# Queries projected as [feature, token] and rotated by three engines, in a fused attention and expert layer on one core

## What is computed

```python
h = concat(tokens_of_image(x), txt)                   # (4, 768, 192)
h = h + attention(layernorm(h))
h = h + ffn(layernorm(h))

# attention: H = 6 heads, DQK = 128, DV = 64
Q = xpos((x @ Wq).reshape(B, T, H, 128), +1)          # x1*cos - x2*sin, x1*sin + x2*cos
K = xpos((x @ Wk).reshape(B, T, H, 128), -1)          # x1, x2: the two halves of the 128 features
V = (x @ Wv).reshape(B, T, H, 64)
out = (Q @ K.T * 128 ** -0.5 * causal_decay_mask) @ V
out = group_norm(out) * silu(x @ Wg) @ Wo
```

## Time and profile before

| | |
|---|---|
| time, median of 3 runs | 920.6 us (918.74 to 922.23) |
| the profiled execution's own time | 925.56 us |
| span from its first to its last instruction | 923.7 us |
| attention, all pairs | until 326 us |
| first matmul of the expert loop | 375 us |
| mean granted TensorE clock | 0.98 of full |

### The profile page before, as it was taken

How to read it: one execution, slowest core, us unless ns; L and a number is a source line. 1 busy time by engine, 2 the same in 40 slices (tenths; PEclk the granted TensorE clock), 3 DMA queues, 4 the chain that set the end, 5 groups by cost and what they waited for, 6 DMA issues and landing times.

```text
span 923.7 us, 16126 instructions
## 1 busy us (share of the span) xinstructions
PE 879.9 (95%) x5422; PEld 399.8 (43%) x5422; DVE 663.0 (72%) x1657; ACT 567.5 (61%) x844; POOL 474.4 (51%) x445
## 2 busy tenths in 40 slices
PE   8899999999999988899799999999999999999997
PEld 3477777777678766222222222222232223222222
DVE  6566555665667577677687888788878887877774
ACT  1121211225332354688788798889988897988784
POOL 0335343333335523476756666757575756574452
PEclk8999999999999999699999999999999999999999
DMA  9600002000000096768687888888988888889773
GB/s 246 230 1 1 2 1 74 1 1 1 1 1 16 15 143 159 188 209 267 181 245 229 254 246 268 242 267 236 295 226 270 247 278 224 276 252 290 243 251 100
DMA packets 89805, 154.14 MB, mean 167 GB/s; under 512 B 30212, under 2 KB 56069, under 8 KB 89330
## 3 DMA queue, kind: packets, MB, share of 16 engines
q1 hardware_dynamic: 89236, 151.48, 54.9%
q10 hardware_dynamic: 486, 1.62, 1.2%
HBM read 138.81 MB, written 15.83 MB: 167 GB/s over the span
## 4 chain that ended last, share of the span: by engine, by line
PE 75%; ACT 8%; DMA 5%; DVE 5%; issue 3%; POOL 2%; SPq 1%; ACTq 0%; DVEq 0%; POOLq 0%
PE ps L854 16%; PE ps L791 15%; PE ps L495 9%; PE ps L503 5%; PE ps L830 5%; PE ps L568 4%; PE ps L560 3%; PE ps L577 3%; DMA w_parts<-wp 2%; ACT ring L1168 2%; PE ps L538 2%; DMA wbc<-w_rows 1%; PE ps L590 1%; PE ps L621 1%; PE ps L642 1%
## 5 line engine op out<-in xcount | busy, mean ns | idle before, releaser
L1829 POOL TENSOR_TENSOR ring<-ring,wbc 128x512 f32<-128x512 f32 x192 | 245.0, 1278 | 160.5 <-ACT ring L1179 147.6
L1628 DVE TENSOR_TENSOR ring<-ps,ring 128x1024 f32<-128x1024 f32 x192 | 234.6, 1222 | 85.8 <-PE ps L830 57.1
L791 PE MATMUL ps<-zst,w1st 99*128 99x512 bf16 x768 | 213.9, 389 | 14.7 <-ACT ring L1168 7.2
L854 PE MATMUL ps<-ring,w2cur 128*32 128x512 f32 x1536 | 205.8, 609 | 0.0
L1168 ACT ACTIVATE ring<-ps 128x1024 f32<-128x1024 f32 x192 | 196.7, 1025 | 4.2 <-PE ps L791 4.1
L1690 POOL TENSOR_TENSOR t<-t 128x768 f32<-128x768 f32 x48 | 87.5, 1834 | 189.7 <-DVE t L1310 189.7
L1181 ACT ACTIVATE ps<-ps 128x512 f32<-128x512 f32 x192 | 113.2, 589 | 61.2 <-PE ps L791 60.7
L1631 DVE TENSOR_TENSOR ring<-ps,wbc 128x512 f32<-128x512 f32 x192 | 130.8, 682 | 1.6 <-DMA wbc<-w_rows 1.5
L1308 DVE TENSOR_TENSOR t<-ps,rope 128x768 f32<-128x768 f32 x48 | 45.7, 953 | 107.1 <-PE ps L503 70.5
L791 PEld LDWEIGHTS ps<-zst,w1st 99*128 99x128 bf16 x768 | 60.9, 98 | 140.8 <-issue 38.3
L1179 ACT ACTIVATE ring<-ps 128x512 f32<-128x512 f32 x192 | 116.3, 606 | 0.0
(11 more groups left out here) (173 smaller groups left out, 1121.4 us busy)
## 6 DMA issues: line engine op xcount, KB each, us to landing
wbc<-w_rows SPq DMA_DIRECT2D x192, 512.0 KB, 5.3
w2cur<-in_w SPq DMA_DIRECT2D x48, 256.0 KB, 4.4
w_parts<-wp SPq DMA_DIRECT2D x72, 64.0 KB, 3.1
zst<-z_parts SPq DMA_DIRECT2D x72, 64.0 KB, 4.7
wst<-w_parts SPq DMA_DIRECT2D x24, 128.0 KB, 3.9
z_parts<-zp SPq DMA_DIRECT2D x6, 384.0 KB, 5.3
wst<-w_parts SPq DMA_DIRECT2D x24, 96.0 KB, 3.7
out_h<-h SPq DMA_DIRECT2D x12, 192.0 KB, 5.0
```

The lines of the kernel that those rows point to most:

```text
L791: return pe.matmul(bank(to), w1st[0:99, 4 * a + j, col:col + P], zst[0:99, (i // 2) % 2, j, :], start=True, stop=True)
L854: mm = pe.matmul(bank(YBANK, 0, 512, 32 * j, 32 * j + 32), w2cur[:, n, j, :], ring[:, (4 * g + j) % RING, :], start=False, stop=(n == 7 an ...
L1628: dve.tensor_tensor(v, ps[:, WBANK * 512:WBANK * 512 + 1024], v, ALU.mult).then_inc(s["duo_done"], 1)
L1829: pool.tensor_tensor(ring[:, slot, :], ring[:, slot, :], wbc[:, g % 4, 1, :], ALU.mult).then_inc(s["tri_done"], 1)
```

## The change

Queries are no longer made as rows of tokens and turned, but come out of the projection as [feature, token]. The weights in the array are now the six 128-column blocks of Wq, and the tokens of both tiles stream through at once, 256 columns a pass. Block e (a head) lies at `query_block(e)` in PSUM: heads 0 to 2 at columns 0 to 767, heads 3 to 5 at 1280 to 2047, so that the rests in the upper half of the array (heads 0 to 2) and those in the lower half (heads 3 to 5) never write into one bank together. For the rests the 64 remaining token features must lie in both halves of the partitions for each tile, so `xn` gets four blocks, the last two with those features written twice, and `xn_turn` makes four transposes.

VectorE calls `rotate_queries` for half 1 first, then for half 0. With features along the partitions, the swap of the feature halves crosses partitions. ScalarE does it with two copies of 64 partitions for each half of the heads (`swap`), VectorE multiplies by the cosines (`rotate_queries`), GpSimd multiplies the swapped ones by the sines (`swapped_queries`) and adds (`rotated_queries`). The rope table of the queries is transposed on the host. `turn`, `keep` and `kT` are for keys alone; `heads` waits for `aq` now. `keys` for x=0 waits for both cosine products, for x=1 for both swaps. `t1`, `t2` and `qkT` are split into parts for queries and keys, and `xnT` moves into the space of `zT`.

```diff
-            def queries(k, x):
+            def query_block(e):
+                return e // 3 * 1280 + e % 3 * 2 * P
+
+            def queries(k, half):
                 pe.wait_ge(s["xn_e"], k + 1)
                 if k > 0:
-                    pe.wait_ge(s["g_out" if x else "v_out"], 2 * k)
-                whole(2 * x, k, x, 0, QK)
+                    pe.wait_ge(s["g_out" if half else "v_out"], 2 * k)
+                for e in range(3 * half, 3 * half + 3):
+                    at = query_block(e)
+                    pe.matmul(ps[:, at:at + 2 * P], wcat[:, 0, e * P:e * P + P],
+                              xnT[:, k % 2, 0:2, :].rearrange("p x n -> p (x n)"),
+                              start=(at % 512 == 0 or e == 3), stop=False, skip_group_check=True)
+
+            def query_rests(k):
+                for n in range(3):
+                    for half in range(2):
+                        e = 3 * half + n
+                        at = query_block(e)
+                        mm = pe.matmul(ps[:, at:at + 2 * P], wcat[D2 * half:D2 * half + D2, 1, e * P:e * P + P],
+                                       xnT[D2 * half:D2 * half + D2, k % 2, 2:4, :].rearrange("p x n -> p (x n)"),
+                                       start=False, stop=True, skip_group_check=True)
+                mm.then_inc(s["q_full"], 1)
...
             def keys(k):
...
                 for x in range(2):
-                    pe.wait_ge(s["rq"], 2 * k + x + 1)
+                    if x == 0:
+                        pe.wait_ge(s["rq"], 2 * k + 2)
+                    else:
+                        pe.wait_ge(s["sq"], 2 * k + 2)
                     whole(2 * x, k, x, QK, QK)
...
             def turn(k, x):
-                pe.wait_ge(s["aq"], 2 * k + x + 1)
                 pe.wait_ge(s["ak"], 2 * k + x + 1)
...
-                for kind in range(2):
-                    for e in range(H):
-                        col = 4 * 512 + (kind * H + e) * P
-                        mm = pe.transpose(ps[:, col:col + P], t1[:, 2 * x + kind, e, :], ident[:, :])
+                for e in range(H):
+                    col = 4 * 512 + (x * H + e) * P
+                    mm = pe.transpose(ps[:, col:col + P], t1k[:, x, e, :], ident[:, :])
...
             def heads(k, x):
                 pe.wait_ge(s["kept"], 2 * k + 2)
+                pe.wait_ge(s["aq"], 2 * k + 2)
...
+            def swap(k, x):
+                hd = DQK // 2
+                src = ps[:, 1280 * x:1280 * x + QK].rearrange("p (h n) -> p h n", n=P)
+                act.wait_ge(s["q_full"], k + 1)
+                if x == 1:
+                    act.wait_ge(s["rq"], 2 * k + 1)
+                if k > 0:
+                    act.wait_ge(s["aq"], 2 * (k - 1) + x + 1)
+                act.copy(s2q[0:hd, x, :, :], src[hd:P, :, :])
+                act.copy(s2q[hd:P, x, :, :], src[0:hd, :, :]).then_inc(s["sq"], 1)
...
+            def rotate_queries(k, x):
+                c = k % CH
+                src = ps[:, 1280 * x:1280 * x + QK].rearrange("p (h n) -> p h n", n=P)
+                dve.wait_ge(s["q_full"], k + 1)
+                if x == 0:
+                    dve.wait_ge(s["sq"], 2 * k + 1)
...
+                dve.tensor_tensor(t1q[:, x, :, :], src, _mid(rope[:, c, 0, :], H), ALU.mult).then_inc(s["rq"], 1)
...
+            def swapped_queries(k, x):
+                pool.wait_ge(s["sq"], 2 * k + x + 1)
...
+                pool.tensor_tensor(s2q[:, x, :, :], s2q[:, x, :, :], _mid(rope[:, k % CH, 1, :], H),
+                                   ALU.mult).then_inc(s["mq"], 1)
+
+            def rotated_queries(k, x):
+                pool.wait_ge(s["rq"], 2 * k + 2)
+                pool.wait_ge(s["mq"], 2 * k + 2)
+                if k > 0:
+                    pool.wait_ge(s["at_full"], 2 * k)
+                pool.tensor_tensor(qT[:, x, :, :].rearrange("p h n -> p (h n)"),
+                                   t1q[:, x, :, :].rearrange("p h n -> p (h n)"),
+                                   s2q[:, x, :, :].rearrange("p h n -> p (h n)"), ALU.add).then_inc(s["aq"], 1)
```

More of the change, by code:

```diff
@@ L155, in fused_layer @@
             state = alloc(region, "state", [P, 2, 2, H, DV])
-            xn = alloc(region, "xn", [P, 3, P])
-            xnT = alloc(region, "xnT", [P, 2, 3, P])
-            xim = t1[0:IMG, 0:2, :, :].rearrange("p a h d -> p (a h d)")[:, 0:B * CIN * IMG]
+            xn = alloc(region, "xn", [P, 4, P])
+            xnT = zT[:, 3 * BLK:5 * BLK].rearrange("p (b x n) -> p b x n", b=2, x=4)
+            xim = t1q[0:IMG, :, :, :].rearrange("p h a n -> p (h a n)")[:, 0:B * CIN * IMG]
             picked = pT[:, :, :, :].rearrange("p a h d -> p (a h d)")[:, 0:B * CIN * IMG]
@@ L486, in xn_turn @@
                 pe.wait_ge(s["xn_d"], k + 1)
-                for n in range(3):
+                for n in range(4):
                     mm = pe.transpose(bank(7, n * P, n * P + P), xn[:, n, :], ident[:, :])
@@ L543, in gates @@
                         mm = pe.matmul(bank(2 + x, g * P, g * P + P), wcat[D2 * x:D2 * x + D2, 1, col:col + P],
-                                       xnT[D2 * x:D2 * x + D2, k % 2, 2, :], start=False, stop=True,
+                                       xnT[D2 * x:D2 * x + D2, k % 2, 2 + x, :], start=False, stop=True,
                                        skip_group_check=True)
@@ L565, in heads @@
                 pe.wait_ge(s["kept"], 2 * k + 2)
+                pe.wait_ge(s["aq"], 2 * k + 2)
                 for e in range(H):
                     col = 4 * 512 + (x * H + e) * P
-                    mm = pe.matmul(ps[:, col:col + P], qkT[:, x, H + e, :], qkT[:, x, e, :], start=True, stop=True)
+                    mm = pe.matmul(ps[:, col:col + P], kT[:, x, e, :], qT[:, e // 3, e % 3 * 2 + x, :], start=True, stop=True)
                 mm.then_inc(s["sc"], 1)
@@ L576, in sums @@
                     o = bank(4 + x, 384 + e * DV, 448 + e * DV) if e < 2 else bank(6, x * 256 + (e - 2) * DV, x * 256 + (e - 1) * DV)
-                    mm = pe.matmul(o, t1[:, 2 * x + 1, e, :], vn[:, x, e, :], start=True, stop=True)
+                    mm = pe.matmul(o, t1k[:, x, e, :], vn[:, x, e, :], start=True, stop=True)
                 mm.then_inc(s["st_full"], 1)
@@ L592, in outputs @@
                             else:
-                                mm = pe.matmul(o, state[:, k % 2, x, 2 * g + e, :], qkT[:, x, 2 * g + e, :],
+                                mm = pe.matmul(o, state[:, k % 2, x, 2 * g + e, :], qT[:, (2 * g + e) // 3, (2 * g + e) % 3 * 2 + x, :],
                                                start=False, stop=True)
@@ L972, in xn_out @@
                     act.wait_ge(s["g_full"], k - 1)
-                act.copy(xnT[:, k % 2, :, :], bank(7, 0, 3 * P).rearrange("p (x n) -> p x n", x=3)).then_inc(s["xn_e"], 1)
+                act.copy(xnT[:, k % 2, :, :], bank(7).rearrange("p (x n) -> p x n", x=4)).then_inc(s["xn_e"], 1)
             def keep(k, x):
@@ L1077, in _ @@
                     keep(p, 1)
+                swap(k, 0)
+                swap(k, 1)
                 if k == 1:
@@ L1279, in xn_make @@
                                       ALU.subtract, ALU.mult)
-                    ins = dve.tensor_scalar(xn[:, 2, D2 * x:D2 * x + D2], h[:, n, P:D], mean[:, n:n + 1],
+                    ins = dve.tensor_scalar(xn[:, 2 + x, :].rearrange("p (a d) -> p a d", a=2), _mid(h[:, n, P:D], 2), mean[:, n:n + 1],
                                             rstd[:, n:n + 1], ALU.subtract, ALU.mult)
@@ L1683, in low_of_w1, with rotated_keys @@
                 pool.tensor_tensor(w1p[:, 2, a:a + BLK], w1f[:, a:a + BLK], w1p[:, 1, a:a + BLK], ALU.subtract)
-            def rotated(k, x, kind):
-                what = "qk"[kind]
-                n = 2 * x + kind
-                pool.wait_ge(s["r" + what], 2 * k + x + 1)
-                pool.tensor_tensor(t1[:, n, :, :].rearrange("p h d -> p (h d)"),
-                                   t1[:, n, :, :].rearrange("p h d -> p (h d)"),
-                                   t2[:, n, :, :].rearrange("p h d -> p (h d)"),
-                                   ALU.add).then_inc(s["a" + what], 1)
+            def rotated_keys(k, x):
+                pool.wait_ge(s["rk"], 2 * k + x + 1)
+                v = t1k[:, x, :, :].rearrange("p h d -> p (h d)")
+                pool.tensor_tensor(v, v, t2k[:, x, :, :].rearrange("p h d -> p (h d)"), ALU.add).then_inc(s["ak"], 1)
+            def swapped_queries(k, x):
+                pool.wait_ge(s["sq"], 2 * k + x + 1)
+                if k == 0 and x == 0:
+                    pool.wait_ge(s["ld_rope0"], 16)
+                if k == 2 and x == 0:
+                    pool.wait_ge(s["ld_rope1"], 16)
+                pool.tensor_tensor(s2q[:, x, :, :], s2q[:, x, :, :], _mid(rope[:, k % CH, 1, :], H),
[3 more added lines that the diff above has]
+                pool.wait_ge(s["mq"], 2 * k + 2)
+                if k > 0:
+                    pool.wait_ge(s["at_full"], 2 * k)
```

(8 more changed lines are left out.)

65 lines of the change are left out of this document (33 added, 32 removed).

## The result

The changed kernel takes 913.2 us, median of 4 runs (910.95 to 914.07), against 920.8 us (918.74 to 922.23) for the kernel before on the same chip: 7.6 us less between the medians, and a ratio of 0.9915 with a 95% interval of [0.9889, 0.9942]. Timed again with the experiments it took 914.8 us against 920.3 for the kernel before, 5.5 us less, ratio 0.9939 [0.9916, 0.9962]. The profiled execution took 912.79 us, its span is 911.0 us.

What follows compares the result with a forecast made beforehand. TensorE's gapless work was taken to bound the attention stage. Terms: -13.3 + 0.5 + 0.95 = -11.9, with 0.6 for loads -11.3 us, giving 914.3 us for the profiled execution and 909.3 for the median; range 904.5 to 916.5.

Steps and rivals of the forecast that it cites:

- case A: Whole kernel: as forecast, 909.3 us, own range 907 to 912.5, with no TensorE gap in the attention stage; chance 0.64.
- B: Attention pairs: the swap chain just misses its cover, 3 to 11 us of the gain go, 913 to 920; chance 0.14.
- Transposes, `xn_turn`: TensorE, each pair: twelve query transposes removed save 1.31 us, a fourth transpose in `xn_turn` costs 0.11; 13.3 us in all.
- Query projection, weight loads: TensorE, query passes and rests: same columns, four more weight loads taken as zero, likely upper bound 1.5 us in all.
- far bounds: Query projection: if none of a weight load hides, four extra loads cost 0.78 us a pair.
- rival C: Query projection: extra weight loads don't hide, costing 4.7 to 9.4 us in all, 914 to 919; chance 0.07.
- The swap chain: Behind the query rests: ScalarE's copies and VectorE's products end at t=2.55, keys x=0 has 0.4 us to spare.
- Rival D: ScalarE's swaps: a 64-partition copy costs double; at 1.6 us each, 27 us lost against 11 gained, 936 us; chance 0.06.
- k=8 and k=9: Work behind the swaps on ScalarE: `wo_pair(0)` 0.6 us late at k=8, `turn_x2(1)` about 0.35 at k=9; loss 0.95 us.
- k=0: First pair: first query pass delayed 0.4 us, keys wait 2.55 us for the swap, their end moves 0.1; loss 0.5 us.
- GpSimd and the hand-over: Query adds end before `heads` needs them; SyncE's loads 0.5 us later; hand-over moves with the stage, +0 us, within 1.
- rival E: Behind the attention stage: the gain is lost at the hand-over as transfers or clock don't follow, 914 to 918; chance 0.09.

Runs made afterwards that it cites:

- turn_twice: Changed kernel with each of a pair's twelve key transposes made twice, to the same place: 928.9 us, 1.0094 of the kernel before.
- pass128: Changed kernel with the queries' whole part projected in 24 passes of 128 columns instead of 12 of 256: 917.0 us in one run.
- straight: Changed kernel whose swap copies stay on the same 64 partitions instead of crossing, so queries are wrong in value: 911.1 us in one run.
- onecopy: Changed kernel with each swap made by one 128-partition copy that doesn't exchange the halves, so queries are wrong: 911.6 us in one run.
- mended: Changed kernel with `wo_pair(0)` behind the sums at k=8 and `x2_out(0)` between the two swaps at k=9: 912.9 us, 0.9916 of the kernel before.
- Fillers: Matmuls with unread results ahead of TensorE's two waits at k=0: in the changed kernel 912.0 us, 0.9882 of the kernel before; also part of `best`.
- zfirst: Changed kernel with GpSimd making the last part of z ahead of the key adds at k=11: 912.8 us, 0.9916 of the kernel before.
- early: Changed kernel with SyncE's expert loads waiting for the sine products instead of the query adds, t2k and s2q exchanged: 914.2 us, 0.9905 of the kernel before.
- best: Changed kernel with all edits of `mended`, `early`, `zfirst` and the fillers at k=0: 906.8 us, 0.9849 of the kernel before.

## Why the prediction came out as it did

The time, 913.2 us, is within the range given and 3.9 us above the point; timed again it was 914.8. Both lie above case A's own 907 to 912.5. The mechanism was that of case A, with small parts of B, and sizes were off. By the steps:

**Transposes, `xn_turn`.** Right: -1.30 and +0.11 us against -1.31 and +0.11 in an ordinary pair, and priced again by `turn_twice`.

**Query projection, weight loads.** Right. The passes cost 0.01 us more and the rests 0.01, so the far bounds and rival C are out, and `pass128` says why: 0.008 us for a load with its instruction. The 0.05 us a pair that I held back for them went elsewhere: the keys' wait took 0.14, and `heads` gave 0.11 that no step of mine had. That an ordinary pair gained 1.16 us where I had 1.15 is luck in this part.

**The swap chain.** Mis-sized. I took 0.70 us from one copy to the next, from the overlap in the earlier trace rows; it was 0.80 to 0.82. The product of half 0 ended at t=2.69 instead of 2.55, and the keys' weight load is due ahead of the end of the heads, by the rows before at t=2.60 and not at 2.98. There were no 0.4 us to spare but, with the release, 0.14 too few. This is rival B at its smallest, 0.8 us in six pairs. Rival D, double cost, is out: `straight` and `onecopy`.

**k=8 and k=9.** Right place and cause, mis-sized. The waits were 1.05 and 0.85 us where the prediction had 0.6 and 0.35, and against a full gain of 1.20 us the two pairs came out 1.13 and 1.10 us short, 1.3 more together than forecast; `mended` wins back 2.4. k=10 kept its 1.19 us of gain. k=11 gained 1.05 instead of 1.31; four of TensorE's other transposes there took 0.66 us in place of 0.44. I didn't follow that further.

**k=0.** Right for the start that its rows came from, missed for the other. The prediction had 0.5 us. With the slow start the pair ends at 43.13 us before and at 43.53 to 43.77 after (four profiles), 0.4 to 0.6 us later; a fifth, `turn_twice`, lost its clock there and ended at 46.77. With the fast start it ends at 41.39 before and at 43.92 to 44.25 after (three profiles), 2.5 to 2.9 us later. Over the two profiles of the kernel before the mean is 42.26 us, over the five of the changed order in the stage 43.86 (43.53 to 44.25), so some 1.6 us, an estimate that hangs on how often each start comes. I had put the query pass on the path in every case; when it ends early, the swap waits for ScalarE's queue, TensorE stands idle for 3.9 to 4.0 us, and its clock falls. Fillers bring 42.44 and 42.21.

**GpSimd and the hand-over.** The adds were in time for `heads` everywhere. The loads of SyncE began 2.1 us behind the stage's end instead of 0.6: I had moved them past the adds, but not the part of z that was moved past them as well, with the store ahead of the loads. It cost nothing measurable (`zfirst`).

**The sum.** For the stage the prediction had -11.75 us for k=1 to 11 and +0.5 for k=0, -11.25. The profiles have -10.55 and +1.6, -8.95. So 2.3 of the 3.9 us are found: 1.2 in the pairs, nearly all of it at k=8 and k=9, and 1.1 at k=0. The rest stays open. From the stage's end to the end of the span it takes 592.9 to 599.6 us in the eleven profiles with the changed order (mean 596.5), and 592.3 to 597.9 in three with the old one (mean 594.6). A loss of 1 to 2 us there (rival E, in small) is neither shown nor excluded, and the intervals of the times are as wide as that.

## What to carry to other kernels

Where TensorE is busy without gaps, a removed instruction is worth its row of the chain at full weight, and the end of a new chain on the other engines must be compared with the next weight load, not with the end of the matmuls before. Don't count on an overlap between two copies because one row shows it for shorter ones. When an instruction is moved in an engine's order, follow each thing that is moved past it to the queues that wait for it, and price a wait with the work behind it. The first pass of a pipeline has other bounds than the rest: read who stands ahead in each engine's queue there, and take it from more than one profile.

## What the runs showed of the hardware

- A ScalarE copy of 768 fp32 elements out of PSUM takes 0.80 us with 64 partitions or 128, across the partition halves or straight. Back to back these stand 0.80 to 0.82 us apart, where 64x256 copies overlapped by 0.10 us.
- Six more fp32 matmuls a pair (twelve instructions, each with its full-height weight load) at equal columns cost 0.09 us.
- Idle for 2.85 us at k=0, TensorE kept 2.4 GHz for its next eight matmuls (2.82 us) in four profiles; in `turn_twice` they took 4.09 behind the same wait, and idle for 3.9 to 4.0 us they took 4.51, mostly at 1.2 GHz, in all three profiles that had it (`early`, `zfirst`, `pass128`; granted clock 0.63 to 0.72 from 32 to 36 us).
- The w_parts store landed 29.5 and 31.5 us behind the stage's end with late loads ahead of it in its queue, and 32.5 us with earlier ones in `zfirst`; in `best`, with loads from 0.1 us on, GpSimd's wait for it ended 30.0 us behind.
